# Gathers paced by the landing of the one but last instead of by pauses, in a four-layer graph network kernel

## The reference

```python
h = jnp.maximum(_layernorm(x, axis=-1), 0.0)
x = x + _L0_gnn_ref(h, ...)        # typed attention: softmax over the edges of a node
h = jnp.maximum(_layernorm(x, axis=-1), 0.0)
x = x + _L1_gnn_ref(h, ...)        # GAT: softmax of leaky_relu(a_src[src] + a_dst[dst])
h = jnp.maximum(_layernorm(x, axis=-1), 0.0)
x = x + _L2_gnn_ref(h, ...)        # segment_sum(h[src], dst) @ weight, by degrees
h = jnp.maximum(_layernorm(x, axis=-1), 0.0)
x = x + _L3_gnn_ref(h, ...)        # exp(clip(score)) attention
```

## Time and profile before

| | us |
|---|---|
| median of three runs | 11216.39 |
| the profiled execution | 11191.52 |
| its span, first to last instruction | 11189.8 |
| GpSimd busy | 8748.9 (78%) |
| TensorE matmuls busy | 6661.3 (60%) |
| VectorE busy | 5435.4 (49%) |
| ScalarE busy | 2291.9 (20%) |
| mean granted clock of TensorE | 0.612 of full speed |

### The profile page before, as it was taken

How to read it: one execution, slowest core, us unless ns; L and a number is a source line. 1 busy time by engine, 2 the same in 40 slices (tenths; PEclk the granted TensorE clock), 3 DMA queues, 4 the chain that set the end, 5 groups by cost and what they waited for, 6 DMA issues and landing times. The chain is left out here.

```text
span 11189.8 us, 165217 instructions
## 1 busy us (share of the span) xinstructions
PE 6661.3 (60%) x36530; PEld 5305.4 (47%) x36531; DVE 5435.4 (49%) x14242; ACT 2291.9 (20%) x6368; POOL 8748.9 (78%) x12683
## 2 busy tenths in 40 slices
PE   5867777777755555555554333333336767776767
PEld 3656556556534444444443333333333555555554
DVE  4266666666666565566554111111113555555555
ACT  1333333333342222222223000000002111111111
POOL 0188888888758888888876888888883888888885
PEclk9966666767765555555556555555555666666667
DMA  3332222222211111111121111111111332222222
GB/s 114 141 87 84 85 85 85 85 86 85 78 43 42 42 42 41 42 42 43 42 49 34 43 43 42 43 43 43 43 43 52 87 86 85 85 85 85 85 85 65
DMA packets 379796, 731.69 MB, mean 65 GB/s; under 512 B 169786, under 2 KB 219249, under 8 KB 373270
## 3 DMA queue, kind: packets, MB, share of 16 engines
q0 software_dynamic: 251264, 621.88, 21.3%
q1 hardware_dynamic: 100906, 98.01, 2.7%
q10 hardware_dynamic: 27500, 10.39, 0.4%
HBM read 652.95 MB, written 76.88 MB: 65 GB/s over the span
## 5 line engine op out<-in xcount | busy, mean ns | idle before, releaser
L467 POOL TENSOR_TENSOR edges_pause<-edges_pause 128x56 f32<-128x56 f32 x6272 | 2094.7, 334 | 120.0
L464 POOL DMA_INDIRECT edges_rows<-gat_rows,edges_idx_r x1568 | 1743.7, 1112 | 326.2 <-issue 301.8
L464 POOL DMA_INDIRECT edges_rows<-conv_rows,edges_idx_r x1568 | 1628.7, 1039 | 331.7 <-issue 320.6
L464 POOL DMA_INDIRECT edges_rows<-kv_typed,edges_idx_r x1568 | 1596.3, 1018 | 332.6 <-issue 313.5
L1005 PE MATMUL edges_ps_sum<-edges_rows,edges_pick 128*128 x3520 | 889.1, 435 | 1580.5 <-POOLq L470 1551.9
L464 POOL DMA_INDIRECT edges_rows<-kv_rows,edges_idx_r x1568 | 1520.5, 970 | 332.1 <-issue 322.7
L615 PE MATMUL edges_ps_sum<-edges_wv,edges_pick 128*128 128x132 f32 x7040 | 1676.2, 410 | 30.1 <-issue 17.6
L615 PEld LDWEIGHTS edges_ps_sum<-edges_wv,edges_pick 128*128 128x128 f32 x7040 | 1433.4, 298 | 368.4 <-issue 340.2
L1005 PEld LDWEIGHTS edges_ps_sum<-edges_rows,edges_pick 128*128 128x128 f32 x3520 | 773.6, 325 | 1695.8 <-issue 1695.7
L1103 PE MATMUL edges_ps_q<-q,edges_pick_t 128*128 x3520 | 751.8, 381 | 726.2 <-DVE edges_prod L1167 644.1
L1025 DVE TENSOR_TENSOR sums<-sums,edges_ps_sum 128x129 f32 x440 | 127.7, 290 | 2038.8 <-PE edges_ps_sum L1005 1684.3
(11 more groups left out here) (343 smaller groups left out, 10567.2 us busy)
## 6 DMA issues: line engine op xcount, KB each, us to landing
kv_typed<-l0pre_out SPq DMA_DIRECT2D x49, 1024.0 KB
edges_rows<-kv_typed,edges_idx_r POOLq DMA_INDIRECT x1568
edges_rows<-gat_rows,edges_idx_r POOLq DMA_INDIRECT x1568
edges_rows<-conv_rows,edges_idx_r POOLq DMA_INDIRECT x1568
edges_rows<-kv_rows,edges_idx_r POOLq DMA_INDIRECT x1568
edges_feat_r<-visit_features ACTq DMA_DIRECT2D x660, 10.0 KB
kv_rows<-l3pre_kv SPq DMA_DIRECT2D x7, 896.0 KB
edges_flag_r<-visit_flags ACTq DMA_DIRECT2D x220, 16.0 KB
```

The lines of the kernel that those rows point to most:

```text
L464: pool.indirect_dma_start(rows[:, k, g * width:(g + 1) * width], None, table, bass.IndirectOffsetOnAxis(ap=idx_r[:, k, g:g + 1], axis=0)). ...
L467: nc.gpsimd.tensor_tensor(pause, pause, pause, ALU.add).then_inc(paused, 1)
```

## The change

In `fetch` the pauses are gone. Each slot has two semaphores in place of one, for the even and the odd gathers of a group. Before its third and fourth gather GpSimd waits until the first or second gather of the same group has landed, before its first and second until the third or fourth of the group before has: at most two gathers are under way. Each of these waits is followed by a `sem_inc`, which before the second gather is `rows_ready` for the group before and otherwise the unused count `slot_free`. The seven words are loaded behind the first gather of every seventh group, for the seven groups that follow; the wait for `used` of every seventh group is thereby made one group earlier, with the wait of the group ahead of it.

In the second pass (`dot=False`) `make_pick` on VectorE is left out. TensorE makes four more small matmuls in `squares`, into a bank `ps_pick` of their own, and ScalarE makes `pick_b` from them as it makes `pick_tb`. `ps_near` has one bank there instead of two, `squares` runs two visits ahead instead of three, and the load of `local` is left out.

```diff
-def fetch(nc, pool, res, rows, table, width, idx_r, idx_in, rows_in, rows_ready, used, slot_free, pause, paused):
-
-    nc.gpsimd.memset(pause, 0.0).then_inc(paused, 1)
+def fetch(nc, pool, res, rows, table, width, idx_r, idx_in, rows_in, rows_ready, used, slot_free):
 
     visits = []
 
     def body(j, k, it):
         if k % HALF == 0:
             pool.wait_ge(idx_in[k // HALF], it * 16 + 16)
-            if known(j, SLOTS):
-                visits[:] = words(pool, res, 3, j - SLOTS, HALF)
-        if known(j, SLOTS):
-            pool.wait_ge(used, at_least_one(pool, visits[k % HALF], NV))
-        pool.sem_inc(slot_free, 1)
+        elif k % HALF == HALF - 1 and known(j + 1, SLOTS):
+            pool.wait_ge(used, at_least_one(pool, visits[HALF - 1], NV))
+        elif known(j, SLOTS):
+            pool.wait_ge(used, at_least_one(pool, visits[k % HALF - 1], NV))
+        back, turn = (k - 1) % SLOTS, it * 32 + (32 if k else 0)
         for g in range(G):
+            if g >= 2:
+                pool.wait_ge(rows_in[k][g % 2], it * 32 + 16)
+            elif known(j, 1):
+                pool.wait_ge(rows_in[back][g], turn)
+            pool.sem_inc(rows_ready if g == 1 and known(j, 1) else slot_free, 1)
             pool.indirect_dma_start(rows[:, k, g * width:(g + 1) * width], None, table,
-                                    bass.IndirectOffsetOnAxis(ap=idx_r[:, k, g:g + 1], axis=0)).then_inc(rows_in[k], 16)
-            pool.wait_ge(paused, j * G + (g + 1))
-            nc.gpsimd.tensor_tensor(pause, pause, pause, ALU.add).then_inc(paused, 1)
-            if g == G - 2 and known(j, 1):
-                pool.wait_ge(rows_in[(k - 1) % SLOTS], it * 64 + (64 if k else 0))
-                pool.sem_inc(rows_ready, 1)
+                                    bass.IndirectOffsetOnAxis(ap=idx_r[:, k, g:g + 1], axis=0)).then_inc(rows_in[k][g % 2], 16)
+            if g == 0 and k % HALF == 0 and known(j + HALF, SLOTS):
+                early = max(SLOTS - 1 - j, 0) if isinstance(j, int) else 0
+                visits[:] = [None] * early + list(words(pool, res, 3, j + 1 - SLOTS + early, HALF - early))
     groups(pool, body)
-    pool.wait_ge(rows_in[SLOTS - 1], NGP // SLOTS * 64)
+    for n in range(2):
+        pool.wait_ge(rows_in[SLOTS - 1][n], NGP // SLOTS * 32)
     pool.sem_inc(rows_ready, 1)
...
-        local, local_in = p.sb("local", [P, NV * G], BF16), p.sem("local_in")
-        ps_near = [p.ps(f"ps_near{j}", [P, GE]) for j in range(2)]
+        local, local_in = (p.sb("local", [P, NV * G], BF16), p.sem("local_in")) if dot else (None, None)
+        near_banks = 2 if dot else 1
+        ps_near = [p.ps(f"ps_near{j}", [P, GE]) for j in range(near_banks)]
+        ps_pick = None if dot else p.ps("ps_pick", [P, GE])
...
-                    if known(u, 2):
-                        pe.wait_ge(pick_tb_done, u - 1)
-                    nc.tensor.matmul(ps_near[s % 2][:], c["col_feat"], feat_r[:, s // 2 % 3, s % 2], start=True,
-                                     stop=True).then_inc(squares_done, 1)
+                    near = feat_r[:, s // 2 % 3, s % 2]
+                    if known(u, near_banks):
+                        pe.wait_ge(pick_tb_done, u + 1 - near_banks)
+                        if not dot:
+                            pe.wait_ge(pick_b_done, u)
+                    mm = nc.tensor.matmul(ps_near[s % near_banks][:], c["col_feat"], near, start=True, stop=True)
+                    if not dot:
+                        for g in range(G):
+                            mm = nc.tensor.matmul(ps_pick[:, g * P:(g + 1) * P], near[:, g * P:(g + 1) * P], c["col_feat"], start=True, stop=True)
+                    mm.then_inc(squares_done, 1)
...
                         act.wait_ge(ref_done, t * 3 + s // SPAN - 2)
-                    nc.scalar.activation(pick_tb[:, s, :], ps_near[s % 2][:], ACT.Relu, bias=1.0, scale=-1.0).then_inc(pick_tb_done, 1)
+                        if not dot:
+                            act.wait_ge(top_part, t * 3 + s // SPAN - 2)
+                    nc.scalar.activation(pick_tb[:, s, :], ps_near[s % near_banks][:], ACT.Relu, bias=1.0, scale=-1.0).then_inc(pick_tb_done, 1)
+                    if not dot:
+                        nc.scalar.activation(pick_b[:, s, :], ps_pick[:], ACT.Relu, bias=1.0, scale=-1.0).then_inc(pick_b_done, 1)
...
-                    if now:
+                    if dot and now:
                         make_pick(now)
-                    if dot and now:
                         multiply_q(now, slot, due)
```

More of the change, by code:

```diff
@@ L484, in softmax_pass @@
         idx_r = p.sb("idx_r", [P, SLOTS, G], I32)
-        pause, paused = p.sb("pause", [P, PAUSE]), p.sem("paused")
         feat_r = p.sb("feat_r", [5, 3, 2, GE], BF16)
@@ L536, in _ @@
                     sp.dma_start(source[:], idx.rearrange("p g t -> p (g t)")).then_inc(source_in, 16)
-                sp.dma_start(local[:], dram["local"]).then_inc(local_in, 16)
+                if dot:
+                    sp.dma_start(local[:], dram["local"]).then_inc(local_in, 16)
                 supply(sp, idx, idx_r, idx_in, rows_ready)
@@ L541, in _ @@
             def _(pool):
-                fetch(nc, pool, res, rows, table, width, idx_r, idx_in, rows_in, rows_ready, wv_done, slot_free, pause[:], paused)
+                fetch(nc, pool, res, rows, table, width, idx_r, idx_in, rows_in, rows_ready, wv_done, slot_free)
             @block.tensor
@@ L627, in body @@
                 def body(i, k, it):
-                    to_square, to_spread, last, ninth = (wide_at(i, k, it, d) for d in (3, 1, -1, -9))
+                    to_square, to_spread, last, ninth = (wide_at(i, k, it, d) for d in (3 if dot else 2, 1, -1, -9))
                     if isinstance(i, int) and i < 0:
@@ L963, in conv_pass @@
         idx_r = p.sb("idx_r", [P, SLOTS, G], I32)
-        pause, paused = p.sb("pause", [P, PAUSE]), p.sem("paused")
         pick, local = p.sb("pick", [P, deep, GE]), p.sb("local", [P, NV * G], BF16)
         ps_sum = [p.ps(f"ps_sum{j}", [P, 512]) for j in range(banks)]
-        rows_in, idx_in = [p.sem(f"rows_in{k}") for k in range(SLOTS)], [p.sem(f"idx_in{k}") for k in range(2)]
+        rows_in, idx_in = [[p.sem(f"rows_in{k}_{n}") for n in range(2)] for k in range(SLOTS)], [p.sem(f"idx_in{k}") for k in range(2)]
         rows_ready, slot_free = p.sem("rows_ready"), p.sem("slot_free")
@@ L987, in _ @@
             def _(pool):
-                fetch(nc, pool, res, rows, table, aw, idx_r, idx_in, rows_in, rows_ready, sum_done, slot_free, pause[:], paused)
+                fetch(nc, pool, res, rows, table, aw, idx_r, idx_in, rows_in, rows_ready, sum_done, slot_free)
             @block.tensor
```

9 lines of the change are left out of this document (4 added, 5 removed).

## The result

The changed kernel takes 12252.73 us (median of four runs, 12249.58 to 12254.04) against 11218.1 us for the kernel before beside it: 1.0921 times as long, with a 95% interval of 1.0902 to 1.094. The forecast was 12520 us, with a range of 11650 to 13200. So direction, size and the main mechanism came out as predicted; the forecast was 267 us too high, its additions were too large, and the step that took the moved one-hots to cost nothing was wrong.

What follows compares the result with a forecast made beforehand. GpSimd's gather pace was taken as the bound. Two rounds of landing plus launch, with additions, gave 28.85 us per four-pass group sum against 25.53; +3.32 times 392 is +1301 us, forecast 12520 us, range 11650 to 13200.

Steps and rivals of the forecast that it cites:

- additions: Per group of four gathers, by pass: lengthening by VectorE and the seven-word load add 0.20, 0.50, 0.40 and 0.15 us.
- The bound: GpSimd's own pace sets each pass's length: 25.53 us summed over four passes, each microsecond worth 392 us.
- Landing, 2.55 and 2.75 us: Gather start to landing seen: 2.55 us in second and third pass, 2.75 us in first and fourth.
- Launch, 0.8 us, from the one row: From the wait's semaphore event to the gather's start: 0.8 us, read from GpSimd's wait for the indices.
- rival of a short launch: Launch behind the event takes only 0.30 us, the sequencer preparing the gather meanwhile: 10950 us; chance 0.06.
- early landing: Landing is seen as soon as the bytes are in, 2.05 and 2.3 us: 11030 us; chance 0.04.
- the late one: A gather with little behind it lands late, 4.4 us, making rounds of 5.2 us: about 18000 us; chance 0.04.
- Rounds of 3.35 and 3.55 us: Landing plus launch in a chain of every second gather; two rounds make a group, 6.70 and 7.10 us.
- The rest of the edit is hidden: Second pass: VectorE loses 309 us, ScalarE gains 259, TensorE about 265, all beside a 666 us wait for rows.
- The sentence on ports: By the Trainium skill's contention rule, VectorE's lengthening of gathers would go with the pauses: some 430 us under the sum.
- The wait never binds: Gathers follow after 1.26 us and compute takes over in the first and fourth pass: 10150 us; chance 0.04.

Runs made afterwards that it cites:

- e4: Changed kernel with the landing wait on the gather itself, not in an event ahead, in the 42 of 392 groups written outside each pass's loop: 12074 us.
- e2: Changed kernel with the old fetch and its pauses, so only the second pass's one-hots are moved off VectorE; on the first chip: 10928 us.
- e1: Kernel before with the new fetch alone; the second pass still makes its one-hots on VectorE: 12388 us.
- e9b: Kernel before, but in the second pass VectorE's one-hots read one operand from PSUM instead of SBUF, and the squares keep one bank: 11012 us.
- e5: Kernel before without its pauses and with nothing in their place; only the old wait, once in four gathers, is left; first chip: 9579 us.
- e11: Kernel before without its pauses and with nothing in their place, a program timed earlier at 9579 us, run again on the third chip: 11783 us.
- e12: Second run, on the third chip, of the kernel before with one-hots moved off VectorE in the second pass and no pauses: 11865 us.

## Why the prediction was right, and where not

- **The bound.** GpSimd's pace set the passes, and the change of its steps gives 1074 of 1058 us of span. Right.
- **Landing, 2.55 and 2.75 us.** Start of a gather to the event behind its landing, at the median: 2.81, 2.61, 2.58 and 2.80 us. Right within 0.06 us, with some luck: 0.35 us of it was a choice between bounds of 0.2 and 0.4, and what the landing was too short (0.03 to 0.06) the launch was too long.
- **Launch, 0.8 us, from the one row.** 0.76, 0.74, 0.74 and 0.73 us at the median. Right, and e4 shows that it hangs on where the wait is written, which the prediction had only inferred. The rival of a short launch fell with it, as did the early landing (the wait would have to end at 2.05 and 2.3 us) and the late one (4.4 us): with at most two gathers under way they land after 2.6 to 2.8 us.
- **Rounds of 3.35 and 3.55 us.** 3.57, 3.36, 3.33 and 3.54 us at the median. Right; this term carries the verdict.
- **The additions, 0.20, 0.50, 0.40 and 0.15 us: mis-sized.** Group less two median rounds: 0.16, 0.22, 0.15 and 0.15 us, 0.68 in place of 1.25. Times 392 the difference is 223 of the 243 us by which the span was over-estimated. In the third pass I let each lengthening count in full; but GpSimd now stands idle where it used to pause, and the gathers mostly start ahead of VectorE's operation, or out of its way: 20 start under it instead of 329, and mean less median is 3 ns instead of 81 ns.
- **"The rest of the edit is hidden": wrong.** I had weighed the moved one-hots by who waits for whom (VectorE, ScalarE and TensorE have room) and so at nothing. They cost GpSimd time as long as they ran on VectorE, which e2, e1 and e9b show. The 0.50 us of the second pass was right for the new wait alone: e1 has 7.34 less the two undisturbed rounds of 6.72, or 0.62. What I had not joined is that the same edit takes these lengthenings away. With the old pace they are worth 262 us, with the new one 136 us by the medians of e1 and the changed kernel, or 0.41 x 392 = 161 us by the pace of the second pass.
- **The sentence on ports.** By the rule of the Trainium skill (SBUF — State Buffer, "Who interferes with whom"), as I read it, the lengthenings would go with the pauses, for 430 us less; they went in the third pass (3 ns of 81 are left) and by more than half in the first (25 of 58 are left), but for another reason. e1's second pass keeps them, with no pauses there at all. So a gather is something that VectorE's second SBUF operand delays; the inference that the making of descriptors is spared doesn't hold here.
- **"The wait never binds", 10150 us.** The size of this rival was wrong. I took 51 us of waiting in the first pass for all that there was to win, because compute seemed near its bound; e5 won 416 us there. But the 51 us came from a trace in which compute was itself held up. With the same code and pace on the first chip, VectorE waits 352 us for rows (e2, against 84 us over the whole run before), and the chip on which e5 won was that one. Elsewhere the first pass without pauses takes longer than before, 2858 us in e11 against 2471, and the whole 11783 us for the same kernel.

## What to carry to other kernels

A wait for the landing of gather n - k sets a pace of (landing + launch) / k where that is over the engine's own: here 1.66 to 1.79 us for k = 2, which bound, and 1.11 to 1.19 us for k = 3, under the engine's 1.26 us. Work this out before choosing k, and write the wait on the gather itself, with nothing between. An operation that reads two SBUF operands lengthens the gathers of GpSimd that start under it; put it on another engine, or one operand into PSUM, even if its own engine is idle. Pauses between gathers may guard against something that one chip never shows: a kernel without them has to be timed on more than one chip before it is believed. And a short wait in a profile shows room on that chip only. Of the versions here that beat the kernel before, only e2 (10928 us, on the first chip) and e9b (11012 us, on the second) keep the pauses; e2 was not run on another.

## What the runs showed of the hardware that I had not expected

- The same program without pauses took 9579 us on one chip and 11783 us on another, with three gathers in flight 9559 and 11840 us, each steady within 0.6%. The median of the kernel with pauses was the same within 0.3% on all.
- Where the kernels without pauses were held up, TensorE's matmuls of one visit stand up to 2.6 us apart with no wait between them (e12), while gathers run without a break. The kernel with pauses has such stands too, 36 us in its first pass, and no time to show for it, because compute waits for rows there.
- A gather starts 0.73 to 0.76 us after the event that stood ahead of it, and 0.46 to 0.52 us sooner if the wait is its own.
- An operand moved from SBUF to PSUM shortened the gathers beside it from 1112 to 1021 ns at the mean. Those that start under an operation with two SBUF operands take 1344 ns, those in whose time it starts 957 ns.
